# Two of four row groups take the second layer before the bias correction in a deformable-attention kernel

## The reference

```python
pos = grid_q[:, :, None, :] - grid_kv[:, None, :, :]
bias = jnp.sign(pos) * jnp.log1p(jnp.abs(pos))
bias = jax.nn.relu(bias @ cpb_w1 + cpb_b1)
bias = jax.nn.relu(bias @ cpb_w2 + cpb_b2)
bias = (bias @ cpb_w3 + cpb_b3).reshape(b, GROUPS, H * W, Hd * Wd)
sim = jnp.einsum('bhid,bhjd->bhij', qh, kh) + bias
attn = jax.nn.softmax(sim, axis=-1)
```

## Time and profile before

| | |
|---|---|
| median of 3 runs | 914.92 us (914.75 to 918.47) |
| the profiled execution's own time | 915.2 us |
| span of its trace | 913.2 us |
| TensorE matmuls busy | 852.4 us, 93% |
| VectorE busy | 721.5 us, 79% |
| ScalarE busy | 641.6 us, 70% |
| GpSimd busy | 62.4 us, 7% |
| mean granted TensorE clock | 0.979 |

### The profile page before, as it was taken

One profiled execution on the slowest core, in us unless ns is written; L12 is line 12 of the kernel. 1 busy time (PEld: TensorE's weight loads), 2 busy tenths in 40 slices (PEclk: granted clock), 3 DMA queues, 4 the chain that ended last, 5 costly groups with the idle time before them and its releaser, 6 DMA issues.

```text
span 913.2 us, 34513 instructions
## 1 busy us (share of the span) xinstructions
PE 852.4 (93%) x15908; PEld 300.2 (33%) x15908; DVE 721.5 (79%) x492; ACT 641.6 (70%) x741; POOL 62.4 (7%) x40
## 2 busy tenths in 40 slices
PE   3299999899999999989999999989999999999996
PEld 1133333233333333324333333423333333333332
DVE  4789699898876689998875878989887768888831
ACT  2367678867776677986776767896777667777762
POOL 2110002310000002040000001140000000000000
PEclk8589999999999999999999999999999999999999
DMA  4301001020110102002020100102020010200001
GB/s 148 91 19 41 13 4 50 8 53 4 45 28 10 50 3 50 8 3 56 3 63 15 49 4 20 34 8 54 4 63 17 2 50 3 73 3 3 3 14 36
DMA packets 23806, 27.48 MB, mean 30 GB/s; under 512 B 15600, under 2 KB 17520, under 8 KB 23664
## 3 DMA queue, kind: packets, MB, share of 16 engines
q1 hardware_dynamic: 23664, 25.29, 10.6%
HBM read 23.05 MB, written 2.10 MB: 28 GB/s over the span
## 4 chain that ended last, share of the span: by engine, by line
PE 83%; DVE 7%; ACT 4%; issue 3%; SPq 1%; DMA 1%; POOL 0%; ACTq 0%; POOLq 0%
PE pair L783 29%; PE scores L797 25%; PE pair L778 10%; PE pair L930 3%; PE scores L807 3%; PE scores L893 3%; PE pair L921 3%; DVE h L576 3%; PE pair L886 2%; ACT h L438 2%; PE pair L905 2%; PE pair L831 1%; PE pair L912 1%; DVE big L680 1%; PE pair L867 1%
## 5 line engine op out<-in xcount | busy, mean ns | idle before, releaser
L438 ACT ACTIVATE h<-pair 128x1024 f32<-128x1024 f32 x512 | 496.3, 1022 | 202.1 <-PE pair L783 200.3
L576 DVE TENSOR_TENSOR h<-hx,hy 128x2048 f32<-128x2048 f32 x256 | 583.3, 2303 | 53.4 <-PE pair L783 53.3
L783 PE MATMUL pair<-h,wts 32*32 32x512 f32 x8192 | 350.9, 599 | 7.5 <-DVE h L576 7.5
L797 PE MATMUL scores<-h,wts 128*32 128x512 f32 x2048 | 274.4, 608 | 0.1
L778 PE MATMUL pair<-fy,u_rows 32*32 32x512 bf16 x4096 | 126.5, 387 | 26.7 <-DMA fy<-fy_dram 17.2
L783 PEld LDWEIGHTS pair<-h,wts 32*32 32x32 f32 x8192 | 134.5, 103 | 25.8 <-DVE h L576 10.5
L797 PEld LDWEIGHTS scores<-h,wts 128*32 128x32 f32 x2048 | 40.4, 108 | 217.0 <-issue 217.0
L778 PEld LDWEIGHTS pair<-fy,u_rows 32*32 32x32 bf16 x4096 | 40.2, 88 | 200.3 <-issue 174.2
L311 POOL TENSOR_TENSOR conv_prod<-qpad,wts 128x288 f32<-128x288 f32 x16 | 21.6, 1379 | 428.9 <-ACT qpad L465 428.9
L418 POOL TENSOR_TENSOR big<-big,hat_x 128x512 f32<-128x512 f32 x16 | 38.0, 2404 | 124.8 <-DVE big L674 124.8
L703 DVE TENSOR_REDUCE neg_max<-pair 128x8 f32<-128x512 f32 x32 | 22.1, 690 | 30.9 <-PE pair L886 30.5
(11 more groups left out here) (87 smaller groups left out, 349.3 us busy)
## 6 DMA issues: line engine op xcount, KB each, us to landing
hx<-features_dram SPq DMA_DIRECT2D x64, 128.0 KB, 2.7
hy<-features_dram SPq DMA_DIRECT2D x64, 128.0 KB, 3.1
att_den<-reciprocals_dram SPq DMA_DIRECT2D x8, 256.0 KB
wts<-weights_dram SPq DMA_DIRECT2D x2, 960.0 KB, 8.0
x<-x_dram SPq DMA_DIRECT2D x2, 512.0 KB, 5.6
fy<-fy_dram SPq DMA_DIRECT2D x64, 6.0 KB
fy<-fy_dram SPq DMA_DIRECT2D x64, 4.0 KB
fy<-fy_dram SPq DMA_DIRECT2D x64, 2.0 KB
```

What stands on the lines that cost most here:

```text
L438: emptied("z", 2 * g + j, act.activation(h2[g % H2_BUFS][:, 2 * j:2 * (j + 1)].rearrange("p r n -> p (r n)"), pair_of("z", 2 * g + j)[:], ...
L576: dve.tensor_tensor(h1[g % H1_BUFS][:].rearrange("p c (y x) -> p c y x", x=W), hx[unit % 2][:, :, t].unsqueeze(2).broadcast_to([128, CT, H ...
L783: ins = pe.matmul(z[r][32 * c:32 * (c + 1)], w(l, "w2")[key[r], key[r]], h1[g % H1_BUFS][key[r], c], start=False, stop=True)
L797: ins = pe.matmul(scores[phase % 2][32 * r:32 * (r + 1)], w(l, "w3")[:, 32 * t:32 * (t + 1)], h2[g % H2_BUFS][:, r], start=t == 0, stop=t ...
```

## The change

The two loops of `layer2` are split in two helpers, `correct(r)` (the four corrections of a row group) and `weigh(r)` (its four second-layer products), which take the start and stop flags as arguments. Row groups 0 and 1 still take the correction first. Row groups 2 and 3 begin with the second-layer product and end with the correction. The order of instructions becomes: turn of the first pair, corrections of 0 and 1, wait for `h1`, turn of the second pair, products of 2 and 3, products of 0 and 1 (then the first pair is filled), corrections of 2 and 3 (then the second pair is filled). The number of instructions, their shapes and their operands stay the same.

```diff
-                for r in range(ROWS):
-                    if r % 2 == 0:
-                        turn("z", 2 * g + r // 2)
+                def correct(r, **ends):
                     y = fy[unit % 2][key[r], t, H // 2 * h:H // 2 * (h + 1)]
                     for c in range(CT):
-                        pe.matmul(z[r][32 * c:32 * (c + 1)], u_rows[l][key[r], 32 * c:32 * (c + 1)],
-                                  y.unsqueeze(2).broadcast_to([32, H // 2, W]), start=True, stop=False)
-                pe.wait_ge(h1_ready, g + 1)
-                for r in range(ROWS):
+                        ins = pe.matmul(z[r][32 * c:32 * (c + 1)], u_rows[l][key[r], 32 * c:32 * (c + 1)],
+                                        y.unsqueeze(2).broadcast_to([32, H // 2, W]), **ends)
+                    return ins
+
+                def weigh(r, **ends):
                     for c in range(CT):
                         ins = pe.matmul(z[r][32 * c:32 * (c + 1)], w(l, "w2")[key[r], key[r]], h1[g % H1_BUFS][key[r], c],
-                                        start=False, stop=True)
-                    if r % 2:
-                        filled("z", 2 * g + r // 2, ins)
+                                        **ends)
+                    return ins
+
+                begins, ends = dict(start=True, stop=False), dict(start=False, stop=True)
+                turn("z", 2 * g)
+                for r in (0, 1):
+                    correct(r, **begins)
+                pe.wait_ge(h1_ready, g + 1)
+                turn("z", 2 * g + 1)
+                for r in (2, 3):
+                    weigh(r, **begins)
+                for r in (0, 1):
+                    ins = weigh(r, **ends)
+                filled("z", 2 * g, ins)
+                for r in (2, 3):
+                    ins = correct(r, **ends)
+                filled("z", 2 * g + 1, ins)
```

## The result

The changed kernel takes 930.91 us (median of 4, 929.65 to 933.42) against 914.84 for the kernel before on the same chip: a ratio of 1.0166, with a 95% interval of 1.0138 to 1.0193. It is slower by 1.7%, where 908.5 us and a gain of 0.7% were forecast. 930.9 also lies outside the range of 901 to 922.

What follows compares the result with a forecast made beforehand. TensorE was taken as the bound (busy 93% of the span). Per phase -0.16 us, times 32 is -5.1, with about 15 waiting steps turned free -6.6: 915.2 to 908.6, given as 908.5; own range 904 to 912, range 901 to 922.

Steps and rivals of the forecast that it cites:

- Case E: Step whose second turn is free at its start: third layer at 1.43 us instead of 1.50, a gain of 0.067.
- The price on the first activation: Row groups 0 and 1 end last, so the activation starts at S + 1.60; the next step's second turn waits until 0.25.
- Case W: Step whose second turn comes 0.25 us late: third layer at 1.51 to 1.52, step 2.52, a loss of 0.03.
- the rival in which the wait doesn't form: Pairs come free in time and all 256 steps gain 0.067 us: 898 us, chance 0.08.
- Step 2 of a phase: Second turn waits 0.5 us in place of 0.3; third layer 1.76 against 1.74, a loss of 0.02.
- The end of the corrections: Late corrections of row groups 2 and 3 after the products in waiting steps: taken as 0.16 us, lower bound 0.
- late corrections pay the queue: Rival: late corrections behind busy tiles enter in two parts 0.19 us apart, 87 steps longer, +16: 925 us, chance 0.15.
- My own sign of being wrong: A third layer more than 1.3 us after line 783 in waiting steps would mean the queue.
- The wait for `h1`: Now before 8 corrections instead of behind 16; VectorE's step is 0.30 us shorter than TensorE's, so costed at 0.
- the loads wait for their row group: Rival: weight loads of late corrections wait for their products, 0.088 us in 87 steps, 7.7: 916 us, chance 0.05.
- Gain and loss cancel: Rival: the tail of waiting steps is 0.06 us longer than taken, 5 us over 87 steps: 914 us, chance 0.20.
- the 0.19 falls away: Rival: products of all row groups interleave without a gap, 0.15 us gained in each of 256 steps: 877 us, chance 0.02.

Runs made afterwards that it cites:

- late_one: The changed kernel with one late correction (row group 2, column tile 0) instead of eight: 913.20 us, 0.9959 of the kernel before.
- one_wait: The changed kernel with the wait for `h1` moved between the corrections of row groups 0 and 1, so no instruction carries two waits: 925.24 us, 1.0109.
- swap: The kernel before, all corrections first, but products in the order 2, 3, 0, 1; VectorE's wait looks at both pairs: 938.65 us, 1.0244.
- late_two: The changed kernel with two late corrections (row group 2, column tiles 0 and 1) instead of eight: 924.72 us, 1.0096 of the kernel before.
- late_one_one_wait: The changed kernel with one late correction instead of eight and the wait for `h1` moved off the second turn: 907.24 us, 0.9921 of the kernel before.
- no_late: The changed kernel without the corrections of row groups 2 and 3; VectorE's wait for a free `h1` buffer looks at both pairs: 914.23 us, 0.9978.
- before_half: The kernel before without the corrections of row groups 2 and 3: 899.94 us, 0.9830.
- first: The changed kernel with late corrections kept but products in the order 0, 1, 2, 3: 942.20 us against 915.35, a single execution.

## Why the prediction was wrong

*Case E* was nearly right where the turn is free: 1.45 to the third layer for 1.43. What I had called hidden, the tail of the corrections, ends just too late (with one late correction it is 1.43, 452.02 to 453.45 in late_one). But a wait under 0.19 was to cost nothing, and in the changed kernel a wait of 0.07 already gives 1.49 (549.55 to 551.04).

*The price on the first activation* was right as a mechanism and too high in size. The second turn waits 0.16 in one_wait, where each instruction has one wait. For 0.25 I had set the activation at S + 1.60; it starts at 1.54 (461.77 to 463.31), and 1.54 + 1.02 + 0.05 - 2.45 = 0.16. The changed kernel's 0.26 agrees with the forecast by luck: 0.09 too much here, and a doubled wait that the forecast didn't have. swap shows what a late first pair costs when all corrections stand ahead: 2.4%. Case W follows case E as forecast, and the rival in which the wait doesn't form (898) is excluded.

*Step 2 of a phase* was added up wrongly. By the prediction's own terms the pair comes free at S + 0.25 + 0.01 + 1.26 + 1.94 + 0.05 = S + 3.51, and step 2 starts at S + 1.52 + 1.00 + 0.59 = S + 3.11, so it waits 0.40 and not 0.5. Step 2 would then have gained 0.08 instead of losing 0.02, and the forecast would have been 3 us lower, further from the result. The trace shows a wait of 0.40 (563.73 to 564.13); the loss comes behind it, 1.42 for 1.25.

*The end of the corrections* is the step that failed: "I take 0.16, since all 16 products are in flight by then and the loads of the corrections are few and short." The runs showed 0.32 to 0.33 (1.41 to 1.42 for 1.09), near the upper bound of 0.35 that I had named. Priced as the prediction prices that rival, 87 steps times the missing 0.17 are 15 us, an estimate, of the 22 between 908.5 and 930.9. It is the rival "late corrections pay the queue" with its 925. I had argued against it from 16 second matmuls that wait without a gap; that those wait so says nothing of matmuls queued behind them. late_one and late_two show the gap: 11.5 us for the second correction. My own sign of being wrong, a third layer more than 1.3 after the second in waiting steps, is what the profile shows.

*The wait for `h1`* was costed at 0 as an edit. It is a second wait on the instruction that has the turn; the program gets an instruction more for it, and where the turn comes late that costs about 0.1: 0.57% here by one_wait (5.2 us), 0.38% between late_one and late_one_one_wait, and 0.76% (7 us) in the kernel before, where the edit moved a little more than that. No rival had it, and it carries the result from the rival's 925 out of the range.

The steps from one run to the next are late_one_one_wait at 0.9921, plus 0.4% for the doubled wait (late_one), plus 1.4% for the second late correction, plus 0.7% for the other six, which is 1.0166. That they add up proves nothing, since each is the difference of two runs; it shows the sizes. And the prices depend on each other through the ring, as the doubled wait's 0.57% with eight late corrections and 0.38% with one show.

*Rivals.* That the loads wait for their row group: two loads of late corrections went ahead of the first (464.91, while the products of row group 2 ran until 465.33), and in late_two both were done before the gap, so it is excluded. "Gain and loss cancel" and "the 0.19 falls away" gave 914 and 877 and are excluded by the time.

*Still open:* why one late correction goes ahead and the next doesn't. The rows give the times, not the mechanism inside the queue. That no_late is as slow as late_one fits the ring, which sets the step in both (2.51 in no_late, 2.49 in late_one at the same place); no run shows it apart from VectorE's doubled wait in no_late.

## What to carry to other kernels

An order that fills idle array tiles can move the end of the tiles that the next engine waits for; follow the ring from that end to the next turn before counting the gain. Where two waits meet at one instruction, count the instructions of the program and give one of the waits another place. And where a ring of buffers sets the step, a shorter tail only makes the next wait longer, as no_late shows. A wait that can't be shortened may be filled with work that needs nothing of the ring, which here gave 0.6% (0.3 to 0.8) for one constant and a guard.

## What the runs showed of the hardware that I had not expected

- Of products queued behind busy tiles of the array, the first starts when its tile is free and those behind it 0.18 later (462.68 and 462.86), even if they are only two bf16 products (0.19 in late_two) and both have their weights.
- Free tiles are reached past blocked ones, but not all: in before_half and first one row group starts 0.07 to 0.08 after the step, while the corrections ahead of it in the program still hold their tiles. That it is a free row group follows from the order of the program and the times; the rows don't name the row group.
- A second wait on a matmul's weight load adds an instruction in each step (34769 for 34513), and where the turn is the later of the two it adds about 0.1 us to the release, 0.26 against 0.16.
